# Tap rows of a sample's first tile made by GpSimd in place of VectorE, in a four-layer fused image kernel

## The reference, cut to what matters

```python
x = x + whiten(gn(x))                  # covariance over all samples, power iteration
x = x + deformable_conv(gn(x))         # below
x = x + window_attention(gn(x))        # 64 windows of 7x7 and a token each, 16 heads, then
                                       # attention between the windows' tokens
x = x + masked_relu_conv3x3(gn(x))

def deformable_conv(x):                # 16 groups of 8 channels, 9 points
    x1 = gelu(layernorm(depthwise3x3(x)))
    offset, mask = x1 @ off_w + off_b, softmax(x1 @ mask_w)
    # for every pixel, group and point: bilinear sample of x @ in_w at the point moved by
    # offset, times mask, summed over the 9 points; then @ out_w
```

## Time and profile before

| | us |
|---|---|
| median of 3 runs (lowest to highest) | 10026.43 (10003.76 to 10063.13) |
| the profiled execution | 10047.3 |
| its span, first to last instruction | 10045.3 |
| TensorE busy | 8162.0 |
| VectorE busy | 7406.0 |
| ScalarE busy | 3949.2 |
| GpSimd busy | 191.2 |

### The profile page before, as it was taken

The page is one execution under the profiler, slowest core; times in us unless marked ns, Lnnn a source line. Parts: engine busy times, 40 slices in busy tenths (PEclk is TensorE's granted clock), DMA queues, the critical chain, the costliest instruction groups (busy, mean ns, idle before and its releaser), DMA issues.

```text
span 10045.3 us, 287502 instructions
## 1 busy us (share of the span) xinstructions
PE 8162.0 (81%) x123582; PEld 4563.3 (45%) x123582; DVE 7406.0 (74%) x8864; ACT 3949.2 (39%) x6124; POOL 191.2 (2%) x253
## 2 busy tenths in 40 slices
PE   6468888887988888798888879888887888888796
PEld 5324445353544535354453534445353444545354
DVE  2488777878777786877778687777868777786863
ACT  0034434253443435334353533434353343535332
POOL 0000000000000000000000000000000000000000
PEclk7579998998989899898999989898998989999898
DMA  4001101111110111111011111101111110111101
GB/s 113 6 13 35 49 20 46 37 38 40 42 44 22 46 31 45 41 37 48 24 46 31 45 41 33 53 22 46 31 45 42 30 54 24 46 31 45 41 25 52
DMA packets 230299, 391.48 MB, mean 39 GB/s; under 512 B 25200, under 2 KB 166480, under 8 KB 221776
## 3 DMA queue, kind: packets, MB, share of 16 engines
q1 hardware_dynamic: 229008, 372.66, 13.3%
HBM read 192.47 MB, written 130.55 MB: 32 GB/s over the span
## 4 chain that ended last, share of the span: by engine, by line
PE 59%; DVE 22%; issue 11%; ACT 6%; DMA 1%; DVEq 1%; SPq 0%; POOL 0%; ACTq 0%; POOLq 0%
PE ps L888 10%; PE ps L689 7%; PE ps L753 7%; DVE arena L1713 4%; PE ps L786 4%; PE ps L988 4%; PE ps L802 4%; PE ps L761 3%; PE ps L978 3%; DVE arena L1768 3%; PE ps L710 3%; PE ps L775 2%; DVE arena L1690 2%; DVE arena L1696 2%; PE ps L922 1%
## 5 line engine op out<-in xcount | busy, mean ns | idle before, releaser
L888 PE MATMUL ps<-arena,ident 64*64 64x512 f32 x5600 | 1739.1, 677 | 745.8 <-DVE arena L1713 745.6
L890 PE MATMUL ps<-arena,ident 48*64 48x512 f32 x5600 | 1742.6, 678 | 0.0
L1713 DVE TENSOR_TENSOR arena<-arena 112x2560 f32<-112x2560 f32 x560 | 1578.2, 2819 | 100.5 <-PE ps L890 93.6
L888 PEld LDWEIGHTS ps<-arena,ident 64*64 64x64 f32 x5600 | 488.6, 148 | 1775.6 <-issue 1764.0
L753 PE MATMUL ps<-arena,wqk 128*128 128x400 f32 x2048 | 909.6, 564 | 152.6 <-DVE arena L1817 119.6
L689 PE MATMUL ps<-vp,convw 128*128 128x448 f32 x2016 | 821.3, 549 | 23.6 <-ACT vp L1310 23.6
L1696 DVE TENSOR_TENSOR arena<-arena 112x576 f32<-112x576 f32 x1008 | 764.2, 758 | 34.9
L802 PE MATMUL ps<-arena 64*64 64x33 f32 x32768 | 656.0, 229 | 127.0 <-issue 71.1
L1808 DVE TENSOR_REDUCE arena<-ps 128x16 f32<-128x800 f32 x512 | 504.9, 986 | 294.9 <-PE ps L775 290.6
L1802 DVE COPY arena<-ps 128x400 f32<-128x400 f32 x512 | 293.0, 572 | 568.2 <-PE ps L753 568.0
L1231 ACT ACTIVATE arena<-ps 112x864 f32<-112x864 f32 x224 | 199.2, 889 | 1299.8 <-PE ps L710 1295.1
(11 more groups left out here) (299 smaller groups left out, 12542.5 us busy)
## 6 DMA issues: line engine op xcount, KB each, us to landing
windows_out<-arena SPq DMA_DIRECT2D x1024, 100.0 KB
arena<-windows_out SPq DMA_DIRECT2D x224, 256.0 KB, 4.2
arena<-windows_out SPq DMA_DIRECT2D x224, 192.0 KB, 3.4
arena<-in_wqk SPq DMA_DIRECT2D x16, 2048.0 KB, 8.5
arena<-in_x_t SPq DMA_DIRECT2D x16, 1568.0 KB, 10.5
arena<-in_x SPq DMA_DIRECT2D x16, 1568.0 KB, 7.3
arena<-arena SPq DMA_DIRECT2D x32, 784.0 KB
out_x<-xb SPq DMA_DIRECT2D x112, 224.0 KB, 2.0
```

Of the source, the lines that this page charges most:

```text
L888: nc.tensor.matmul(ps[half, 3, :], ident[0:SLOT, 0:SLOT], prod[0:SLOT, ring(c, dy), dx, :], start=(s < 2), stop=(s >= TAPS - 2), skip_grou ...
L890: mm = nc.tensor.matmul(ps[half, 4, :], ident[SLOT:PT, SLOT:], prod[SLOT:PT, ring(c, dy), dx, :], start=(s < 2), stop=(s >= TAPS - 2), ski ...
L1713: V.tensor_tensor(prod[0:PT, ring(c, dy), :, :].rearrange("p k (n e) -> p k n e", e=CG), taps.to_broadcast([PT, SHIFTS, N64, CG]), for_tap ...
```

## The change

For the first tile of each sample all three rows of taps are made by GpSimd. VectorE signals `rw_s` ("mask is in the hats") in pair 29 and makes no row for that tile. GpSimd makes the rows between zeroing the first buffer and zeroing the second, in the same twelve instructions, each behind a wait for the one before. The counts of VectorE's own semaphore steps are adjusted.

```diff
-DVE_PRE, DVE_MAIN, DVE_BLK, DVE_END = 6 + 8 * DW_BLOCKS, 105, 69, 46
+DVE_PRE, DVE_MAIN, DVE_BLK, DVE_END = 6 + 8 * DW_BLOCKS, 96, 69, 46
+POOL_ROWS = 9
...
+            def first_rows_of_taps(n):
+                rows = Chain(pool, t_rows)
+                rows.turn(n, POOL_ROWS)
+                pool.wait_ge(k_z.sem, k_z.at(n, 1))
+                alone(pool)
+                pool.wait_ge(rw_s.sem, rw_s.at(n, 1))
+                alone(pool)
+                for bb in range(3):
+                    if bb:
+                        pool.wait_ge(k_s.sem, k_s.at(n, bb))
+                        alone(pool)
+                    rows.step(nc.gpsimd.tensor_tensor(
+                        om_first[0:PT, :].rearrange("p (a n) -> p a n", a=3), hat_first[0:PT, :, 0, :],
+                        hat_first[0:PT, bb, 1:2, :].to_broadcast([PT, 3, HN]), ALU.mult))
+                    alone(pool)
+                    for aa in range(3):
+                        k5 = kw[0][0:PT, :].rearrange("p (y x n) -> p x y n", y=5, x=5)[:, aa:aa + 3, bb:bb + 3, :]
+                        ins = nc.gpsimd.tensor_tensor(k5, k5, om_first[0:PT, aa * HN:(aa + 1) * HN].rearrange(
+                            "p (x y n) -> p x y n", x=3, y=3), ALU.add)
+                        if aa == 2:
+                            ins.then_inc(k_s.sem, 1)
+                        else:
+                            rows.step(ins)
+                            alone(pool)
+                rows.end()
+
             def zero_taps(i, n):
                 for u in range(2):
+                    if u:
+                        first_rows_of_taps(n)
                     if i is not None:
                         pool.wait_ge(s_p.sem, s_p.at(i, PAIRS if u else PAIRS - 4))
...
                 elif s == OFF_AT + 4:
                     rows_by_mask(n, 0)
-                elif OFF_AT + 5 <= s < OFF_AT + 7:
-                    by_row(n, 0, s - (OFF_AT + 5))
+                    ownm.settle()
+                    dve.sem_inc(rw_s.sem, 1)
...
                         if dy == 0:
-                            by_row(n, c, 1 if c else 2)
+                            if c:
+                                by_row(n, c, 1)
```

More of the change, by code:

```diff
@@ L295, in build @@
         d_init, d_a, d_cov, d_pow, d_pre, d_main, d_blk, d_end = (sem(f"dve_own_{k}") for k in range(8))
-        t_main = sem("act_own_main")
+        t_main, t_rows = sem("act_own_main"), sem("pool_own_rows")
         a_xt = [sig("a_xt0", 16), sig("a_xt1", 16)]
```

## The result

The changed kernel took 10189.42 us in the median of 4 runs (10155.43 to 10227.11), the kernel before 10038.73 (10003.76 to 10063.13, 4 runs): 1.0154 times as long, 95% interval 1.0105 to 1.0203, some 151 us more. The profiled execution took 10182.9 us, 135.6 more than that of before.

A forecast was written before the change was run, and what follows sets the result against it. The end of the first tile's third tap row, which releases SyncE's weights and tokens, was taken to set each stage. 15 x 9.1 + 10 = 146 us on the median of 10026 gave 10172 us, range 10035 to 10240.

The forecast's parts named there:

- The third row sets the stage, through SyncE's queue, a microsecond for a microsecond in 15 samples: SyncE issues weights and tokens after the third tap row; each microsecond later costs one in each of 15 samples.
- A row on GpSimd takes 8.19 us, 2.5 memset passes: GpSimd's tap row: one instruction of 3.69 us, three of 1.30 and four handovers of 0.15.
- the three-pass end: Ceiling for GpSimd's two-input instructions, two reads and a write without overlap: 1.54 us for 576 elements, 4.41 for 1728.
- two passes: Lower middle for GpSimd's instructions, only the reads adding: 6.8 us a row; with contention +76 us in all.
- the prediction's estimate of 25: GpSimd's 12 instructions by the Trainium skill's add times, 4497 ns against VectorE's 2293: 25 us without handovers.
- Two readers exclude each other, 5.6 us a sample: VectorE's first two multiplies, 2 x 2.82 us, delay GpSimd's rows by their full length, since both read SBUF.
- K3 9.1 us late: End of the first tile's third tap row at 4650.5 instead of 4641.5, given as 9.1 us later.
- VectorE's first multiply 4.8 us earlier, worth nothing: After the attention, it starts at 4629.6 instead of 4634.38; VectorE reaching the token wait earlier gains nothing.
- Sample 0 loses 10 us: Without attention beside it, its rows last until 637.5 while its third multiply started at 627.50: 10 us, once.
- The moved parts are free: Zeroing the second tap buffer and ScalarE's tile 1 hats come later, but cost nothing under the tokens' transfer.
- Signs: Expected in the new profile: weights issued 30 us after the hats, token idle 13 or more, TensorE's pause 9 longer.

The follow-up runs named there:

- row order: Kernel before, with row 2 of the first tile made ahead of the first multiply instead of behind it: 9963.49 us, ratio 0.9929.
- a wait in the queue: Kernel before, with SyncE also waiting for the second multiply before issuing weights and tokens: 10072.05 us, ratio 1.0035.
- tokens first: Kernel before, with the window tokens issued ahead of SyncE's wait for the third row: 9899.69 us, ratio 0.9867; on the changed kernel 10060.22 us, ratio 1.0028.

## Why the prediction was right

It gave 10172 us, range 10035 to 10240, and +146; measured were 10189 and +151. The mechanism holds. That the two sums agree within 5 us is luck: the measured interval runs from 105 to 204 us, and the terms as measured (below) add up to 158.

- *The third row sets the stage, through SyncE's queue, a microsecond for a microsecond in 15 samples.* The path is shown, by four gates moved in different ways (row order, a wait in the queue, GpSimd's rows with and without the meeting), and by taking it away (tokens first). The rate of one for one holds within the intervals upwards; downwards the kernel gained more, 71 us for 41.
- *A row on GpSimd takes 8.19 us, 2.5 memset passes.* It takes 3.83 + 3 x 1.40 + 4 x 0.18 = 8.75 where nothing meets it. The instructions were forecast at 3.69 and 1.30, the handover at 0.15. Three rows are 1.7 us longer than forecast. The value lay in the middle of bounds that reached from one pass to three, and the three-pass end (4.41 and 1.54) was too high. The step from 576 to 1728 elements gives 2.1 ns an element, 2.5 memset passes of 0.83 as chosen; no row had shown that the reads add and the write in part, so the choice was in part luck: two passes would have made the sum 76 us, three 214. The twelve instructions come to 24.1 us without handovers, beside the prediction's estimate of 25.
- *Two readers exclude each other, 5.6 us a sample.* 4.9 measured: the whole of both multiplies was put on GpSimd, but at the first meeting GpSimd is ahead and VectorE bears 2.1 us of it. Where the meeting is removed the kernel is 63 us faster. The rule of the Trainium skill (SBUF — State Buffer, "Who interferes with whom") is borne out in both directions: VectorE first, GpSimd's instruction takes 6.37 for 3.83; GpSimd first, VectorE's takes 4.93 for 2.82.
- *K3 9.1 us late* (its own terms give 9.0). The gate moved by 9.95 in the sample shown, 9.8 in the mean: 1.7 more for the rows, 0.7 less for the meeting.
- *VectorE's first multiply 4.8 us earlier, worth nothing.* In the sample shown it starts 10.7 us after the hats for 14.3, but that sample is a late one: over the 15 it is 9.4 to 11.4, mean 9.9, for 14.4, so 4.6 earlier. It was worth nothing: delaying it by some 16 us in an experiment cost nothing in these samples either.
- *Sample 0 loses 10 us.* Its third multiply starts 31.8 us after the hats for 20.4: 11.5. With 15 x 9.8 that makes 158.
- *The moved parts are free.* The second buffer is zeroed and ScalarE's hats of tile 1 start when the third row ends, and both are done within the tokens' transfer (GpSimd's at 4716.6, ScalarE's six at 4718.7, the tokens at 4723.9). In the kernel before the second buffer was zeroed at 4619.08, not at 4630 as the prediction has it; nothing hangs on that.
- *Signs.* L476 about 30 us after the hats: 31.3. Idle before the tokens 13 or more: 17.08. TensorE's pause before the third multiply's sums was to grow by 9 us: it grew from 9.21 to 20.84 in the sample shown, by 11.6, since TensorE also ends the second multiply's sums earlier against the hats. All its waits for multiplies grew from 745.6 to 958.5 us, 13 a sample.

## What to carry to other kernels

Work taken from a busy engine is worth only what it takes from the wait that ends last, and here that wait was a DMA held back by a semaphore of the moved work itself; follow each signal of a moved piece to its other waiters before counting the busy time saved. On a queue that issues in order, a small load that is needed first goes ahead of a large one that has to wait: that alone was worth 1.3%, and nothing of it shows in busy time. No kernel here gained by work moved to GpSimd: three rows cost 149 us, and one row, which met nothing of VectorE's that was slowed, gained nothing; VectorE's next row waited 1.78 us for it. Whether a piece that nobody waits for would pay was not tried.

## What the runs showed of the hardware

- GpSimd's two-input instructions on fp32 took 1.40 us for 576 elements and 3.83 for 1728 in each of 112 partitions, 2.1 ns an element from one size to the other, nearly twice VectorE's 0.758 and 1.95 us, and 0.18 us from the end of one to the start of the next that waits for it.
- Not only instructions with two tensor inputs waited for GpSimd. VectorE's L1908, one tensor of 128 x 8 elements and constants, took 3.37 us for 0.17 beside a GpSimd multiplication. L1837 and L1853, which read PSUM, and L1839 and L1855, which read PSUM for one of two inputs, were not stretched, though some of them lie beside GpSimd's rows at every seam: the 512 of L1839 in the changed kernel took 0.990 to 0.993 us each.
- Tokens (two loads of 64 KB) landed 7.4 us after their issue in the median, behind a load of 2048 KB in the same queue, and after 2.2 us ahead of it.
